# A fused attention and feed-forward layer: normed groups transposed in halves on row tiles, another rule for the ring of banks, another order on every queue

## The reference

```python
mod = (silu(c) @ wmod).reshape(8, 6, 1, 128)          # sa, ca, ga, sb, cb, gb
h = layernorm(x) * (1 + ca) + sa
x = x + ga * attention(h)                              # retention: 8 heads, keys of 64, values of 128
h = layernorm(x) * (1 + cb) + sb
x = x + gb * ffn(h)
# attention: q, k rotated; scores = (q k^T / 8) * decay^(t - s), causal; o = scores v
#            o = groupnorm(o) * gn_weight + gn_bias; out = (o * silu(h Wg^T)) Wo^T
# ffn:       xr, xk = mixes of h with the token before it
#            out = sigmoid(xr Wr^T) * (relu(xk Wk^T)^2 Wv^T)
```

## Time and profile before

| | before |
|---|---|
| median of 3 runs | 761.41 us (760.25 to 762.11) |
| the profiled execution | 763.29 us |
| its span, first to last instruction | 761.5 us |
| PE busy | 734.5 us (96%) |
| DVE busy | 600.1 us (79%) |
| POOL busy | 586.4 us (77%) |
| ACT busy | 457.5 us (60%) |
| mean granted TensorE clock | 0.991 |

### The profile page before, as it was taken

How to read it: one execution, slowest core, us unless ns; L and a number is a source line. 1 busy time by engine, 2 the same in 40 slices (tenths; PEclk the granted TensorE clock), 3 DMA queues, 4 the chain that set the end, 5 groups by cost and what they waited for, 6 DMA issues and landing times.

```text
span 761.5 us, 29079 instructions
## 1 busy us (share of the span) xinstructions
PE 734.5 (96%) x12093; PEld 645.9 (85%) x12093; DVE 600.1 (79%) x1273; ACT 457.5 (60%) x889; POOL 586.4 (77%) x641
## 2 busy tenths in 40 slices
PE   5788999999999999999999999999999999999996
PEld 3567888898888889888888889888888888888875
DVE  6877687879879787887978788797887878787545
ACT  4255656666666566657556665655656565656664
POOL 3748777897878887798878978788877977777651
PEclk9799999999999999999999999999999999999999
DMA  9422222112123122222312212231321222122100
GB/s 327 126 52 51 44 43 51 31 37 58 26 47 72 41 54 50 44 51 43 72 40 61 43 40 55 51 71 23 72 46 41 58 44 57 24 58 43 37 15 28
DMA packets 66402, 42.46 MB, mean 56 GB/s; under 512 B 38232, under 2 KB 55904, under 8 KB 66272
## 3 DMA queue, kind: packets, MB, share of 16 engines
q1 hardware_dynamic: 65552, 39.81, 22.4%
q10 hardware_dynamic: 720, 0.80, 0.3%
HBM read 11.22 MB, written 4.20 MB: 20 GB/s over the span
## 4 chain that ended last, share of the span: by engine, by line
PE 91%; DVE 3%; ACT 1%; issue 1%; DMA 1%; POOL 1%; SPq 0%; DVEq 0%; POOLq 0%; ACTq 0%
PE ring L308 52%; PE outs L308 14%; PE O_E L308 13%; PE ring L323 8%; PE O_O L308 2%; PE ring L347 2%; DMA N<-in_w_qkT 1%; DMA k_odd<-rot_k 1%; POOL gn_rstd L1183 0%; DVE N L961 0%; POOL y L1190 0%; DVE swapped L910 0%; DVE turned L905 0%; ACT y L729 0%; ACT normed L624 0%
## 5 line engine op out<-in xcount | busy, mean ns | idle before, releaser
L1190 POOL TENSOR_TENSOR y<-y,gate 128x512 f32<-128x512 f32 x123 | 154.9, 1280 | 25.2 <-ACT y L676 25.1
L308 PEld LDWEIGHTS outs<-wo_gated,y 128*128 128x128 f32 x992 | 127.7, 191 | 10.1 <-POOL y L1190 1.6
L1173 POOL TENSOR_TENSOR rot_k<-rot_k,sin_k 128x256 f32<-128x256 f32 x128 | 108.4, 867 | 34.7 <-DVE sin_k L927 34.7
L308 PE MATMUL outs<-wo_gated,y 128*128 128x128 f32 x992 | 131.3, 275 | 1.1 <-POOL y L1190 1.0
L1183 POOL TENSOR_TENSOR gn_rstd<-gn_var,minus_half 128x8 f32<-128x8 f32 x64 | 105.3, 1645 | 5.0
L954 DVE TENSOR_REDUCE gn_sum<-N 128x4 f32<-128x512 f32 x118 | 75.4, 681 | 40.8 <-ACT N L664 40.8
L1167 POOL TENSOR_TENSOR qT<-qT,swapped 128x512 f32<-128x512 f32 x64 | 83.0, 1297 | 19.9 <-DVE swapped L910 19.6
L676 ACT ACTIVATE y<-ring,gn 128x512 f32<-128x512 f32 x126 | 90.9, 776 | 4.8 <-PE ring L323 4.8
L637 ACT ACTIVATE v_odd<-ring 128x512 f32<-128x512 f32 x64 | 38.3, 598 | 91.5 <-PE ring L308 91.5
L934 DVE TENSOR_TENSOR A<-ring,consts 128x256 f32<-128x256 f32 x128 | 47.9, 416 | 51.0 <-PE ring L308 50.9
L948 DVE TENSOR_TENSOR S<-ring,S 128x512 f32<-128x512 f32 x112 | 76.9, 686 | 8.9 <-PE ring L308 6.9
(11 more groups left out here) (167 smaller groups left out, 2105.1 us busy)
## 6 DMA issues: line engine op xcount, KB each, us to landing
v<-v_odd SPq DMA_DIRECT2D x128, 128.0 KB, 2.3
k_odd<-rot_k SPq DMA_DIRECT2D x128, 64.0 KB, 2.2
X<-in_x SPq DMA_DIRECT2D x16, 256.0 KB, 3.3
out<-X SPq DMA_DIRECT2D x15, 256.0 KB, 3.1
key_tables<-in_const SPq DMA_DIRECT2D x7, 256.0 KB, 8.3
rotary_q<-in_const_q SPq DMA_DIRECT2D x2, 512.0 KB, 8.5
gates<-stored_rows SPq DMA_DIRECT2D x8, 128.0 KB, 3.2
N<-in_w_qkT SPq DMA_DIRECT2D x1, 512.0 KB, 5.0
```

The source lines that it names most:

```text
L308: return e.matmul(o, lhsT, rhs, start=start, stop=stop, skip_group_check=True)
L1173: done = e.tensor_tensor(turned[:, n, :, :], turned[:, n, :, :], sin[:, n, :, :], op)
L1190: e.tensor_tensor(y[:, n % NY, :], y[:, n % NY, :], gate[:, n % 2, :], ALU.mult).then_inc(sem["y"])
```

## The change

`transpose_n` takes two banks, one for each half of the tokens, and makes eight transposes of 64 tokens in place of four of 128; the two that read them, `full_h` and `modulate2`, become two instructions each, of 256 columns. `take_bank` no longer looks at when a bank was taken, but at that plus a number for what it is taken for (`HOLD`). On PE, `project_v(even)` and `project_k` now come ahead of the even `project_out`, so that this one and the odd `project_out` of the next step stand side by side; `project_ffn_out` comes ahead of `project_q`. Lines of the other queues are reordered, some by a step.

```diff
+HOLD = {'mod_cols': 5, 'mod_gates': 2, 'nT0': 2, 'nT1': -1, 'q': 3, 'k': 1, 'v': 0, 'kT': 0, 'S': 2, 'gate': 0, 'n': 1, 'r': 3, 'ffn_k': -2, 'ffn': 4}
-        taken = [0] * RING
+        taken, takes = [0] * RING, [1]
# take_bank
-                    taken[n] = max(taken) + 1
+                    taken[n] = max(takes) + HOLD.get(what[0], 0)
+                    takes.append(max(takes) + 1)
# free_heads
-                    taken[n] = max(taken) + 1
+                    taken[n] = max(takes)
# transpose_n
-                bank = take_bank((f"nT{which}", g), free[which])
+                pair = [take_bank((f"nT{which}", half, g), free[which]) for half in range(2)]
...
-                    done = e.transpose(bank[:, j * P:(j + 1) * P], normed[:, j, :], ident)
+                    done = transpose_halves(pair, j * HALF, normed[:, j, :])
# PE, order of a step
+                for g in due(step - 13, GC, LAST - 1):
+                    project_ffn_out(g)
                 for m in due(step + 4, 1, NCHUNK):
                     project_q(m)
-                for g in due(step - 13, GC, LAST - 1):
-                    project_ffn_out(g)
+                for _ in due(step, 1, 1):
+                    mod_gates()
                 for i in due(step + 1, 1, NCHUNK):
                     project_v(i, 1)
...
-                for _ in due(step, 1, 1):
-                    mod_gates()
+                for i in due(step + 1, 1, NCHUNK):
+                    project_v(i, 0)
                 for g in due(step + 5, GC, NGROUP):
                     transpose_n(g, 0)
+                for i in due(step + 2, 1, NCHUNK):
+                    project_k(i)
+                for i in due(step - 1, 1, 2, 1):
+                    free_heads(i)
                 for g in due(step - 10, GC, LAST):
                     transpose_n(g, 1)
                 for i in due(step - 5, 1, NCHUNK - 1):
                     project_out(2 * i)
-                for i in due(step + 1, 1, NCHUNK):
-                    project_v(i, 0)
-                for i in due(step + 2, 1, NCHUNK):
-                    project_k(i)
# ACT, modulate2
-                e.activation(h2T[:, half, 1:1 + W], bank_of["nT1", g], ACT.Identity, bias=mod_cols[:, 2, b:b + 1],
-                             scale=mod_cols[:, 3, b:b + 1]).then_inc(sem["h2T"])
+                parts = in_halves(by(GC, h2T[:, half, 1:1 + W]))
+                for n in range(2):
+                    done = e.activation(parts[:, n, :, :], by(GC, bank_of["nT1", n, g][:, 0:W // 2]), ACT.Identity,
+                                        bias=mod_cols[:, 2, b:b + 1], scale=mod_cols[:, 3, b:b + 1])
+                done.then_inc(sem["h2T"])
# DVE, full_h: the same with two tensor_scalar
# DVE, order: norm_stats(g, 1) from the end of a step to the start of the next, split_mix(g) between
# the two masks, ffn_product and mod_gates ahead of rotate_q, full_h between the two norm_heads
# POOL, order of a step
+                for m in due(step + 6, 1, NCHUNK):
+                    rotate_q(m)
                 for g in due(step - 8, GC, LAST):
                     mix_delta(g)
...
                 for i in due(step + 4, 1, NCHUNK):
                     rotate_k(i)
+                for g in due(step + 11, GC, NGROUP, 1):
+                    norm_rstd(g, 0)
+                for g in due(step - 11, GC, LAST - 1):
+                    ffn_out(g)
...
                 for i in due(step - 2, 1, NCHUNK - 1):
                     gate_head(2 * i)
+                for g in due(step - 6, GC, LAST):
+                    norm_rstd(g, 1)
                 for i in due(step - 2, 1, NCHUNK - GC):
                     gate_head(2 * i + 1)
                 for i in due(step + 2, 1, NCHUNK):
                     head_rstd(i)
...
-                for g in due(step + 11, GC, NGROUP, 1):
-                    norm_rstd(g, 0)
# SP, order of a step
-                for g in due(step + 62, GC, NGROUP, 7):
+                for g in due(step + 63, GC, NGROUP, 7):
                     load_x(g)
...
-                for i in due(step + 55, 1, NCHUNK):
+                for i in due(step + 54, 1, NCHUNK):
                     swap_v(i)
+                for _ in due(step + 53, 1, 1):
+                    store_gates()
+                for b in due(step + 53, 1, 2):
+                    load_gates(b)
                 for i in due(step + 55, 1, NCHUNK):
                     swap_k(i)
```

More of the change, by code:

```diff
@@ L542, in _ @@
                     project_ffn_k(g)
+                for i in due(step - 6, 1, NCHUNK - 1):
+                    project_out(2 * i + 1)
                 for _ in due(step - 68, 1, 1):
                     project_ffn_k(LAST - 1)
-                for i in due(step - 6, 1, NCHUNK - 1):
-                    project_out(2 * i + 1)
                 for i in due(step - 5, 1, NCHUNK):
@@ L796, in _ @@
                     norm_apply(g, 0)
-                for g in due(step + 6, GC, NGROUP, 1):
-                    round_h(g)
                 for i in due(step + 2, 1, NCHUNK):
@@ L804, in _ @@
                     scale_head(2 * i + 1)
+                for g in due(step - 9, GC, LAST):
+                    round_mix(g)
+                for _ in due(step, 1, 1):
+                    round_w_k()
             act_k(LAST - 1)
@@ L889, in full_h @@
                 at.wait_ge("hT_lo", g)
-                e.tensor_scalar(h_full[:, :], bank_of["nT0", g], mod_cols[:, 1, b:b + 1], mod_cols[:, 0, b:b + 1],
-                                ALU.mult, ALU.add).then_inc(sem["h_full"])
+                parts = in_halves(by(GC, h_full[:, :]))
+                for n in range(2):
+                    done = e.tensor_scalar(parts[:, n, :, :], by(GC, bank_of["nT0", n, g][:, 0:W // 2]), mod_cols[:, 1, b:b + 1],
+                                           mod_cols[:, 0, b:b + 1], ALU.mult, ALU.add)
+                done.then_inc(sem["h_full"])
             def low_h(g):
@@ L1070, in _ @@
             for step in steps:
+                for _ in due(step - 3, 1, 1):
+                    split_w_k()
+                for g in due(step + 8, GC, NGROUP, 1):
+                    norm_stats(g, 0)
                 for b in due(step - 6, CB, B):
                     ffn_weights(b)
-                for g in due(step + 8, GC, NGROUP, 1):
-                    norm_stats(g, 0)
-                for i in due(step - 6, 1, NCHUNK - 1, NCHUNK - GC):
-                    last_gate(2 * i + 1)
                 for g in due(step - 11, GC, LAST):
                     mix_shift(g)
+                for g in due(step - 9, GC, LAST):
+                    norm_stats(g, 1)
                 for i in due(step, 1, NCHUNK):
                     mask(i, 1)
+                for i in due(step - 5, 1, NCHUNK - 1, NCHUNK - GC):
+                    last_gate(2 * i + 1)
+                for g in due(step - 12, GC, LAST):
+                    split_mix(g)
                 for i in due(step, 1, NCHUNK):
@@ L1088, in _ @@
                     add_state(i)
+                for g in due(step - 13, GC, LAST - 1):
+                    ffn_product(g)
+                for _ in due(step, 1, 1):
+                    mod_gates()
                 for m in due(step + 4, 1, NCHUNK):
                     rotate_q(m)
[L1091 to L1096 removed]
+                for i in due(step - 1, 1, NCHUNK):
+                    norm_heads(i, 0)
                 for g in due(step + 5, GC, NGROUP, 1):
                     full_h(g)
[L1099 to L1100 removed]
                 for i in due(step - 1, 1, NCHUNK):
@@ L1106, in _ @@
                     residual(g)
-                for g in due(step - 8, GC, LAST):
-                    norm_stats(g, 1)
-                for g in due(step - 11, GC, LAST):
-                    split_mix(g)
-                for _ in due(step - 1, 1, 1):
-                    split_w_k()
+                for _ in due(step + 4, 1, 1):
+                    split_w("w_v", raw_vc, wv)
             last_heads(0)
@@ L1250, in _ @@
                     head_rstd(i)
-                for b in due(step - 1, CB, B, 1):
+                for b in due(step, CB, B, 1):
                     gate_weights(b, 0)
-                for g in due(step + 11, GC, NGROUP, 1):
-                    norm_rstd(g, 0)
-                for _ in due(step - 3, 1, 1):
+                for _ in due(step + 3, 1, 1):
+                    split_w_g()
+                for _ in due(step - 2, 1, 1):
                     gate_weights(0, 1)
+                for b in due(step - 3, CB, B, 1):
+                    gate_weights(b, 1)
             last_rstd(0)
@@ L1326, in _ @@
             for step in steps:
-                for g in due(step + 62, GC, NGROUP, 7):
-                    load_x(g)
                 for g in due(step + 38, GC, LAST):
                     store(g)
-                for i in due(step + 55, 1, NCHUNK):
+                for g in due(step + 63, GC, NGROUP, 7):
+                    load_x(g)
+                for b in due(step + 61, CB, B, 2):
+                    load_gates(b)
```

(11 more changed lines are left out.)

52 lines of the change are left out of this document (15 added, 37 removed).

## The result

The changed kernel takes 765.38 us (median of 4 runs, 764.52 to 765.67), the kernel before in the same comparison 761.64 us (4 runs, 760.25 to 762.11). The ratio is 1.0051 with a 95% interval of 1.003 to 1.0072: slower by half a percent, above the 0.3% that can be told from no change. The profiled execution took 765.51 us, with a span of 763.7 us and a mean granted clock of 0.99. The forecast was 762.8 us, the range 757 to 768; slower had a chance of 0.36.

What follows compares the result with a forecast made beforehand. PE was taken to bound the dense stretch, 80 to 712 us. Terms +4.0, 0, -1.0, +0.6, -2.7, -0.8, +0.8 and +0.5 sum to +1.4 us, added to the median 761.41: 762.8 us, range 757 to 768.

Steps and rivals of the forecast that it cites:

- Part 1: Normed transposes in halves on PE, dense stretch: 0.59 us a group in place of 0.44, 27 groups, +4.0 us.
- Parts 2 and 3: Output products side by side 0; bank ring and queue order in the dense stretch -1.0 and +0.6 us.
- Part 4: The ramp, first 80 us: -2.7 and -0.8 from waits gone, +0.8 and +0.5 from later work.
- tail: The last 50 us, a chain through ACT, POOL and PE: 0, bounds -1 and +1 us.
- within 0.3%: The forecast case that the kernel's time stays within 0.3% (2.3 us), no change that can be told: chance 0.38.
- the -2.7: In the ramp, state(2) no longer waits for the odd keys, as swap_k(2) is issued ahead of swap_v(2): -2.7 us.
- rival in which row tiles pay off: Borders of the half transposes are hidden: -5.4 us in place of +4.0, 753.4 us; chance 0.10.
- the edge: In the dense stretch, transpose_k no longer waits for project_k's bank: 27 steps at 0.04, -1.0 us, bound -2.7.
- POOL's new order: norm_rstd ahead of and between gates: +0.6 us with other order edges; rival with a wait each group, 768.2 us, chance 0.16.
- transpose_k(5) ... -0.8: In the ramp, transpose_k(5) no longer waits for a bank of project_k(6), as it takes others: -0.8 us.
- The two losses: In the ramp, full_h behind norm_heads delays transpose_k(4), +0.8 us; project_v(even) of chunk 0 waits for project_k(0)'s bank, +0.5.
- the ramp gives nothing back: In the ramp, another late transfer or a later clock rise removes the -2.7 and -0.8: +4.9, 766.3 us; chance 0.20.

Runs made afterwards that it cites:

- second profile of before: The kernel before, unchanged, profiled once more: this execution took 761.49 us, with a span of 759.7 us.
- first profile: The kernel before, unchanged, in the profiled execution that the prediction was made from: 763.29 us, with a span of 761.5 us.
- halves_two_places: The changed kernel with each block of half transposes cut in two, full-array work between: 787.17 us, ratio 1.0332 to the kernel before.
- cand1: The changed kernel's order with the old full-array transposes, HOLD with q 2 and k 2, counted from the thirtieth take: 761.16 us, ratio 0.9998 to the kernel before.
- before_sp: The kernel before with only SP's order from the change: 760.82 us, ratio 0.9988 to the kernel before.
- ffn_k_ahead: The changed kernel with project_ffn_k(14) ahead of the last odd project_out, as in the kernel before: 766.46 us, ratio 1.0066 to the kernel before.
- modulate_14_ahead: The changed kernel with ACT's modulate2 of the last group ahead of the gates: 765.77 us, ratio 1.0066 to the kernel before.
- full_again: The changed kernel with the old full-array transposes into one bank, ring rule and order kept: 765.08 us, ratio 1.0044 to the kernel before.
- halves_alone: The kernel before with only the transposes in halves, old ring rule and old order: 785.62 us, ratio 1.0314 to the kernel before.
- old_ring: The changed kernel with the old rule of take_bank, without HOLD: 782.27 us, ratio 1.028 to the kernel before.
- full_fit_modulate: full_fit with ACT's modulate2 of group 14 ahead of the gates: 765.07 us, ratio 1.0057 to the kernel before.
- full_fit: full_again with two numbers of HOLD changed (nT0 3, ffn_k 1): 765.62 us, ratio 1.0064 to the kernel before.

## Why the prediction was right, and where it was not

**The range and part 1 held; the ramp was the failed step.** Term by term, against the second profile of before:

| term | predicted | measured |
|---|---|---|
| Part 1, halves | +4.0 | +3.9 to +4.2 |
| Parts 2 and 3, outputs, ring, order | -0.4 | -2.1, and +0.5 in single waits |
| Part 4, ramp | -2.2 | +1.0 |
| tail | 0 | +0.5 |
| sum | +1.4 | +4.0 |

That the time fell into the range owes something to luck: the ramp missed by 3.2 us one way, parts 2 and 3 by 1.2 us the other. The point forecast, 762.8 us, missed by 2.6, and the case with the highest single chance, "within 0.3%", did not come.

Part of the miss is in how the sum was set up. It took its gain from a profiled execution of 763.29 us and added it to the median, 761.41 us. From the first profile to the changed kernel the span grew by 2.2 us (ramp -1.5, dense stretch +2.6, tail +1.1), near the +1.4; the late landing that the -2.7 was to win back is in that profile and not in the median.

- *Part 1* was right, in mechanism and size. Its three prices, taken from `turn_heads` and the state's tiles, all showed: 0.06 a pair (halves_two_places), 0.35 for entering and leaving (the same run), 0.59 a group (the profile after). cand1 gives the sum: 44.93 - 44.61 = 0.32 us in four chunks, 13 times in the dense stretch, 4.2 us. Group by group, from the start of the even `project_v` to that of `turn_heads`, the first norm's is 0.14 us dearer than in cand1 and the second's 0.16 (medians of 12 and 13): 0.30 in four chunks, 3.9 us. So nearly all of it is PE's own work, and the second reading instruction on DVE and ACT costs nothing there, as forecast. The Trainium skill, TensorEngine Tiling (Array Packing), section Key Properties, has it that a change of tiling mode drains the engine; by that rule a border costs time, and the trace agrees, with 0.35 us for entering and leaving. The rival in which row tiles pay off is refuted: a pair is indeed cheaper by 0.05 us than a full transpose, four of them give 0.20, and the borders take 0.35.
- *Parts 2 and 3* had the right sign and were too small. With the old transposes on both sides, before takes 579.49 us for the dense stretch and cand1 577.42: -2.1, where -0.4 was forecast in all, -1.0 for the edge with a bound of -2.7. cand1 has two other numbers in `HOLD`, so for the changed kernel the -2.1 is an estimate: its +2.6, less 4.2 for the halves and 0.5 for the single waits. The term was mis-sized by its count. In before_sp 15 steps show `turn_heads` up to 0.06 us longer (0.9 us together) and 34 steps `transpose_k` up to 0.05 longer (1.7 us); the prediction had taken 27 at 0.04. In the changed kernel 53 of 54 steps take 0.55 and 0.34 us, so the edge is gone; the earlier trace rows happens to show a step of before that had neither. One step of the changed kernel in PE's timeline:

```profile
412.18 0.71 PE L325 MATMUL ring<-consts,N 64*128 64x64 f32 x16
412.73 0.41 PE L325 MATMUL ring<-consts,rot_k 64*128 64x64 f32 x8
413.08 0.32 PE L310 MATMUL O_E<-v,A 64*64 64x128 f32 x1
```

- *POOL's new order* opened no wait in a group. In the dense stretch PE waited once, 0.42 us for a mask at 641.84 us, and its weight queue once more, 0.30 us at 461.25; `norm_rstd` ahead of the gates and behind one costs no wait there. These two make up the 0.5 us of single waits, near the +0.6 in size; that POOL's order caused them is not shown.
- *Part 4* failed, and with it the forecast of "within 0.3%". The step was: "even with 4.09 us it lands before 44. **-2.7**". What the runs showed in its place: the 4.09 us were one landing (2.24 in the second profile), so no more than 0.8 to 1.0 us was there to win; and the new order of the two copies pays for its gain at state(2) with state(0). The prediction had it that both copies gain, and did not follow the values of chunk 0 (before_sp, 0.01 us at chunk 4 in sum). "transpose_k(5) ... -0.8" failed too: it still waits, 0.69 us, for `sin_k`. The step "by the new rule it takes others" was a slip: followed through, the new rule gives it the bank of `project_k(6)` again. The two losses were right: `h_full` behind `norm_heads` was priced at +0.8, and from `scores(3)` to `scores(4)` it takes 8.80 us against 8.06; the bank of `project_k(0)` was priced at +0.5, and of the 1.1 us that it costs at `scores(0)` (27.70 against 26.64) 0.4 are left at `scores(1)` (36.46 against 36.08). State(2) brings 0.6 (`scores(3)` at 51.00 against 51.38, from 43.19 against 42.96 at `scores(2)`), and a late mask ahead of state(4) takes 0.5.
- *The rival "the ramp gives nothing back"* is the one that came: 766.3 us, against 765.38 measured. One of its reasons, another late transfer, is shown for state(0) in before_sp. The other, a clock that rises later, is not: the low level ends between 32 and 33 us in before and changed alike. In the changed kernel itself state(0) doesn't wait, because `scores(0)` is already late by more.
- *The tail* is 0.5 us longer than in the second profile of before, 1.1 longer than in the first. One group's border shows in it: `scores(63)` stands 9.50 us behind `scores(62)`, 9.35 before. The rest is open; none of three edits brought it back.

What stays open beyond that: how much of a ramp is chance. The two profiles of before differ by 2.5 us there; three profiles with the changed kernel's order in that stretch took 101.89, 102.06 and 102.45 us to chunk 8 (the changed kernel, ffn_k_ahead, modulate_14_ahead). So the +1.0 is +1.0 to +1.6 against the second profile of before, and -1.5 to -0.9 against the first. The dense stretch, which repeats to 0.01 us in before and to 0.4 us in those three (582.07, 581.72, 581.76), carries the account.

## What to carry to other kernels

Price a block on another tiling mode with its borders, from start to start of its neighbours: a gain of 0.05 us a pair needs more than seven pairs before it pays the 0.35 us of one entry and one exit (an estimate from these rows), so such blocks belong next to others of the same mode. A bank more for one product changes every later take of a ring; build the pure version of the ring before judging the edit by an undo, as full_again and cand1 differ by 3.4 us in the dense stretch with the same tiles. And before a forecast builds on a wait in a ramp, look whether the transfer behind it took its usual time in that execution: 4.09 us stood beside a median of 2.2 for the same copies.

## What the runs showed of the hardware

- A copy of 64 KB from SBUF to SBUF, issued at 42.05 and 42.14 us in two executions of the same kernel, with the same work around it, took 4.09 and 2.24 us from issue to landing. The median of 128 such copies was 2.2 us in both, the longest 4.09 and 3.5.
- Entering 64 x 128 row tiles from the full array and leaving them again costs 0.35 us on PE with four pairs of 64-token transposes in a block and with two (0.34 and 0.35 us for the second pair of borders in halves_two_places).
- Which bank a product takes is worth more than the product's own form: some 17 us (halves_alone) and 10.3 us (old_ring) of waiting in the dense stretch, against 3.9 to 4.2 us for the tiles.
- The granted clock was 0.50 for 10 us in the ramp of before and of the changed kernel, from about 22 us on. Where the same order ran with 0.77 and 0.84 in place of 0.50 and 0.73 (22 to 30 and 30 to 40 us: full_fit_modulate, full_fit), the ramp was 1.4 us shorter.
